# Graph gather summed in pairs of steps: two matmuls into one PSUM bank, one add per pair, the edge list padded per tile to an even number of steps

## The chip, the cores and the metric

The kernel runs on one core of a Trainium2 chip. The metric is the device time of one execution in microseconds (us); a lower time is better.

## The reference, cut to what matters

One block of a graph transformer on 12500 nodes of 256 features, fp32. The part that the change touches is the sum of messages over the 200000 edges of the first graph:

```python
xn = _layernorm(x, axis=-1)
# GCN: h = relu(batchnorm(xn @ w1.T + b1)); xw = (h @ w2.T + b2) @ w_gcn.T
msgs = xw[src] * norm[:, None]
out = jax.ops.segment_sum(msgs, dst, num_segments=n) + b_gcn
# x = x + GCN(xn) + linear attention(xn), then a GAT-gated mixture of 4 experts is added
```

`dst` is sorted. The linear attention beside the GCN (projections of `xn`, a small state per head, a second projection) and the preparation of the second graph's edge list are computed in the same stage of the kernel as this sum.

## The kernel before, in words

The program is a row of blocks, with a barrier between them: edges and first half (`load_edges`, `first_half`), rows of the table (`table_rows`), the gather with the attention (`gather_mix`), `second_norm`, the experts with the second graph (`gat_experts`, `gat_finish`), `finale`. Only `gather_mix` does other work after the change.

Nodes lie in NT = 100 tiles of TN = 125. `table_rows` writes the scaled rows `xw` to `table` in DRAM, and makes the list of **steps**. A step is 128 edges of one tile. A tile has as many steps as its edges need (`nch`, L750 and L751), and the steps of all tiles stand behind each other; `S_GCN` (L44) is the number that suffices for any edge list, rounded up. For each step there are a column of 128 source rows (`gcn_srcT`), a column of 128 destinations less the tile's first node (`gcn_dstT`) and the tile's number (`gcn_tiles`). A step of the list beyond the last edge takes its 128 pairs from a tail that `load_edges` wrote with source 0 and destination -1 (L345 and L346): it gathers row 0 of the table 128 times, and its one-hot matrix is all zeros.

`gather_mix` takes the steps in groups of 4, and two of them make a slot (`SLOTS = S_GCN // 2`, 832). The order on each engine is written out slot by slot:

- POOL (L919 to L926) issues one indirect DMA per step, 128 rows of 1 KB from `table` into `g_rows`, a ring of 4 groups. Before a group it waits until PE has done the group 4 back (`mm_s`).
- DVE `build(g)` (L1259) makes the four one-hot matrices `g_hot` of a group by comparing `gcn_dstT` with a ramp, one group ahead.
- PE `gathered(p)` (L984 to L995) waits for the one-hots and the rows of a group, and for `add_s` of the slot 4 back, and multiplies one-hot by rows for the two steps of the slot, each into its own half of one of four banks of `g_ps`. One increment of `mm_s` follows.
- DVE `add(p)` (L1263 to L1271) reads the two tile numbers into registers, waits for `mm_s`, and adds the two halves one after the other to the accumulator row `acc` of their tiles. The second add waits for the first, since both may go to the same tile.

The attention is woven in by slot number: the first half (queries, keys and values, state) takes 13 slots for each of 25 blocks (slots 0 to 336), the second half 8 slots per block from slot 337 (to 546), and the counts of the second graph's nodes (`degrees`, L1339 and L1083) 4 slots per round, to about slot 806. A sorting network of the second graph's edges runs on DVE (L1367 and L1368) beside these. In a slot DVE does `build` (every second slot), `add`, and then its piece of the other work, strictly in this order. In the first half PE's product for keys and values (L1013) waits for DVE's `k_sum` (L1281) of the block before; in the second half PE's products L1053 and L1070 wait for DVE's L1330 and L1323.

The few lines of the slot loop on DVE:

```python
for p in range(SLOTS):
    if p % 2 == 0 and p // 2 + 1 < S_GCN // 4:
        build(p // 2 + 1)
    add(p)
    ...
```

Of the kernel before, what the change touches and what calls it, by code (L numbers as in the profile page):

```python
# [10 lines left out]
ALU = mybir.AluOpType  # L11
# [4 lines left out]
D = 256  # L16
P = 128
TN = 125
NT = N // TN
# [11 lines left out]


ROUND = BATCH * HALVES


def steps_for(edges, unit):


    most = (edges + NT * P * unit) // P
    return -(-most // ROUND) * ROUND  # L40


UNIT_GCN = 1
S_GCN = steps_for(E_GCN, UNIT_GCN)  # L44
G_GCN = -(-S_GCN // P)
NE, FF = 4, 512
# [106 lines left out]
def where(eng, flag):  # L153

    return nullcontext() if flag is None else eng.If(eng.value_load(flag[:], min_val=0, max_val=1))
# [139 lines left out]
def scatter_unsorted(nc, K):  # L295

    with ExitStack() as ctx:
        scatter = Scatter(Mem(nc, ctx), "gc", K.gcn_pairs, GCN_P, K.gcn_place, K.gcn_pay)
        with nc.Block() as block:
            @block.gpsimd  # L300
            def _(pool):
                with where(pool, K.unsorted):
                    scatter.run(pool, 0, GCN_C // ROUND)

# [300 lines left out]
def table_rows(nc, K, A):  # L605
# [3 lines left out]
    with ExitStack() as ctx:  # L609
# [12 lines left out]
        G = G_GCN  # L622
        wide = P * UNIT_GCN
        ch_start, ch_end, base = (m.sb("t_" + s, [P, NT]) for s in ("start", "end", "base"))
# [24 lines left out]
        with nc.Block() as block:  # L649
# [79 lines left out]
            def _(dve):  # L729
# [13 lines left out]
                def done(ins):  # L743
                    n[0] += 1
                    ins.then_inc(t_s, 1)
                    dve.wait_ge(t_s, n[0])
# [3 lines left out]
                done(dve.tensor_scalar(nch_i[:], K.cnt[:], 1.0 / wide, (wide - 1) / (2.0 * wide), ALU.mult, ALU.add))  # L750
                done(dve.tensor_scalar(nch[:], nch_i[:], 1.0, float(UNIT_GCN), ALU.max, ALU.mult))  # L751
                done(dve.tensor_tensor_scan(ch_end[:], nch[:], nch[:], 0.0, ALU.add, ALU.bypass))
# [58 lines left out]
def gather_mix(nc, K, A):  # L811
# [9 lines left out]
    RING, HB = 4, 16  # L821
    with ExitStack() as ctx:
        m = Mem(nc, ctx)
        rows = m.sb("g_rows", [P, RING, 4, D])
        hot = m.sb("g_hot", [P, 3, 4, TN])
        ps = m.ps("g_ps", [P, 4, 2, D])
        hot_s, mm_s, add_s = (m.sem("g_" + s) for s in ("hot", "mm", "add"))
        got = [m.gather_sem(f"g_got{h}") for h in range(RING)]

# [65 lines left out]
        q = slice(0, TN)  # L895
# [18 lines left out]
        with nc.Block() as block:  # L914
# [69 lines left out]
            def _(pe):  # L984
                def gathered(p):
                    g, j = divmod(p, 2)
                    if j == 0:
                        pe.wait_ge(hot_s, g + 1)
                        pe.wait_ge(got[g % RING], 64 * (g // RING + 1))
                    if p >= 4:  # L990
                        pe.wait_ge(add_s, 2 * p - 6)
                    for b in range(2):
                        mm = pe.matmul(ps[q, p % 4, b], hot[:, g % 3, 2 * j + b], rows[:, g % RING, 2 * j + b],  # L993
                                       start=True, stop=True, skip_group_check=True)
                    mm.then_inc(mm_s, 1)  # L995

                def project_q(k, o):
# [135 lines left out]
                for p in range(SLOTS):  # L1133
                    gathered(p)
                    k, r = divmod(p - MIX1, W1)
                    if 0 <= k < NB:
                        if r in (0, 2):
                            project_q(k, r // 2)
                        elif r in (3, 5, 7, 9):
                            project_kv(k, (r - 3) // 2)  # L1140
                        elif r in (6, 8, 10, 12):
                            accumulate(k, (r - 6) // 2)
                    middle(p - MIX1 - NB * W1)
                    k, r = divmod(p - MIX2, W2)
                    if 0 <= k < NB:
                        second(k, r)
                    if 0 <= p - HIST - W3 < half * W3:
                        degrees(p - HIST - W3)
                    if p % 2 == 0:
                        next(order, None)  # L1150
# [103 lines left out]
            def _(dve):  # L1254
# [6 lines left out]
                                      ).then_inc(hot_s, 1)  # L1261

                def add(p):  # L1263
                    tiles = [dve.value_load(K.gcn_tiles[0:1, 2 * p + b:2 * p + b + 1], min_val=0, max_val=NT - 1)
                             for b in range(2)]
                    dve.wait_ge(mm_s, p + 1)
                    for b in range(2):
                        a = K.acc[q, bass.ds(tiles[b], 1), :].rearrange("p a f -> p (a f)")
                        if p or b:
                            dve.wait_ge(add_s, 2 * p + b)  # L1270
                        dve.tensor_tensor(a, a, ps[q, p % 4, b], ALU.add).then_inc(add_s, 1)  # L1271

                def q_sum(k, o):
                    n = k * KC + o
# [214 lines left out]
# [4 lines that stand above are left out]
                    k, r = divmod(p - MIX1, W1)  # L1493
                    if 0 <= k < NB:
                        if r in (1, 3):
                            q_sum(k, r // 2)
                        elif r in (4, 6, 8, 10):
                            k_sum(k, (r - 4) // 2)
                    middle(p - MIX1 - NB * W1)
                    k, r = divmod(p - MIX2, W2)  # L1500
                    if 0 <= k < NB:
                        second(k, r)
                    numbers(p - HIST + 3)
                    if 0 <= p - HIST < half * W3:
                        degrees(p - HIST)
                    if p % 2 == 0:
                        next(order, None)
                    if p >= HIST - 40 and p % 2 == 1:
                        next(after, None)
# [778 lines left out]
def program(nc, A):  # L2288
    with ExitStack() as ctx:
# [23 lines left out]
        with ExitStack() as c1:  # L2313
            m1 = Mem(nc, c1)
            K.gcn_srcT = m1.sb("gcn_srcT", [P, G_GCN * P], U32)
            K.gcn_dstT = m1.sb("gcn_dstT", [P, G_GCN * P])
            K.gcn_tiles = m1.sb("gcn_tiles", [1, G_GCN * P], I32)
            K.acc = m1.sb("acc", [P, NT, D])
            with ExitStack() as c2:
                m2 = Mem(nc, c2)  # L2320
                K.both = m2.sb("w_both", [P, KC, D])
                K.b_both = m2.sb("b_both", [P, D])
                K.hmv = m2.sb("hmv", [P, KC, 2])
                K.cnt = m2.sb("cnt", [P, NT])
                with ExitStack() as c6:
                    m6 = Mem(nc, c6)
                    K.degree = m6.sb("degree", [P, NT])
                    K.base = m6.sb("base", [P, NT])
                    load_edges(nc, m6, K, A)
                    with ExitStack() as c7:  # L2330
                        K.gcn_place = Mem(nc, c7).sb("gcn_place", [P, GCN_C], U32)
                        places(nc, K, "gc", GCN_P, GCN_C, K.gcn_tile, K.cnt, K.base, K.gcn_place, K.unsorted)
                        scatter_unsorted(nc, K)
                    first_half(nc, K, A)
                table_rows(nc, K, A)
            gather_mix(nc, K, A)
            second_norm(nc, K, A)
# [43 lines left out]
```

## Time and profile before

| What | Value |
|---|---|
| median of 3 runs | 6648.84 us (6631.96 to 6654.02) |
| the profiled execution | 6612.06 us, span 6610.4 us |
| stage of the gather, from DVE's first add to its last | 734 to 3368 us |
| PE, DVE, POOL busy over the span | 67%, 39%, 44% |
| mean granted TensorE clock | 0.737 |

The profiled execution is 37 us under the median and 20 us under the lowest of the three runs. Times are us from the span's start. Shares over the whole span say little here, since each stage has its own bound; the stage is read by itself, and inside it by the work that is woven in. PE rows carry the start of a matmul, their ends are modelled. A wait for several semaphores stands under the one that came last by the trace; "issue" is time in which the engine waited for nothing that the profile shows, "remote" a release that the profile could not place.

### The profile page before, as it was taken

Reading aid. Unit: us, or ns where it says so; the run is one execution under the profiler, and the core shown is the slowest. Engines: PE = TensorE matmul, PEld = TensorE weight load, DVE = VectorE, ACT = ScalarE, POOL = GpSimd, SP = SyncE. Lnnn points to the kernel's source line nnn. Section 1 sums busy time; section 2 is a strip of 40 time slices with the busy share of each in tenths; the row PEclk is TensorE's granted clock in tenths of the full one; section 3 lists DMA queues with packets and bytes.
Section 4 is the critical chain, followed back from the end, with each engine's and each line's share of the span. In section 5 each row is a group of like instructions: output and inputs, shape, how many; then the busy total and the mean of one; then the engine's idle time right before and its main releaser. Section 6 shows DMA issues by size and latency. Waiting matters only on the chain. (4 is left out here: it accounts for less than half of the span.)

```text
span 6610.4 us, 50389 instructions
## 1 busy us (share of the span) xinstructions
PE 4430.7 (67%) x14755; PEld 3046.5 (46%) x14755; DVE 2593.8 (39%) x5223; ACT 758.7 (11%) x1439; POOL 2901.8 (44%) x2919
## 2 busy tenths in 40 slices
PE   6998777888788887777754325764775485451264
PEld 6887544444455555666644113442443253230143
DVE  5555565565554445555554000220221121113244
ACT  1112311212000000000011001110111011010111
POOL 0000466666655556777710772334434523552300
PEclk8667989888776777777755557876876697675687
DMA  2112433333444443333465211221221121211265
GB/s 68 50 50 51 138 114 113 109 116 112 114 129 124 128 116 93 92 90 91 88 132 148 37 9 41 50 50 25 50 50 26 35 64 27 45 31 39 54 174 140
DMA packets 241863, 531.52 MB, mean 80 GB/s; under 512 B 73332, under 2 KB 147415, under 8 KB 234822
## 3 DMA queue, kind: packets, MB, share of 16 engines
q1 hardware_dynamic: 121909, 293.42, 16.4%
q0 software_dynamic: 119696, 235.05, 15.1%
q8 instruction: 115, 1.88, 0.1%
q14 instruction: 143, 1.17, 0.1%
HBM read 377.97 MB, written 150.28 MB: 80 GB/s over the span
## 5 line engine op out<-in xcount | busy, mean ns | idle before, releaser
L923 POOL DMA_INDIRECT g_rows<-table,gcn_srcT x1664 | 1707.0, 1026 | 915.9 <-issue 460.9
L1768 POOL DMA_INDIRECT n_rows<-gtab,so_own x1122 | 1081.7, 964 | 1246.6 <-DVEq L1885 905.5
L993 PE MATMUL g_ps<-g_rows,g_hot 128*125 128x256 f32 x3328 | 1082.3, 463 | 262.8 <-DVE g_hot L1259 172.0
L1716 PE MATMUL p_py<-f_w,f_hh 128*125 128x256 f32 x2688 | 723.0, 407 | 791.8 <-issue 791.6
L1271 DVE TENSOR_TENSOR acc<-acc,g_ps 125x256 f32 x1664 | 700.6, 421 | 1004.1 <-PE g_ps L993 339.1
L1716 PEld LDWEIGHTS p_py<-f_w,f_hh 128*125 128x125 f32 x2688 | 539.2, 201 | 994.9 <-issue 932.3
L993 PEld LDWEIGHTS g_ps<-g_rows,g_hot 128*125 128x125 f32 x3328 | 702.8, 229 | 514.2 <-issue 210.4
L1909 DVE TENSOR_TENSOR p_ob<-p_py,p_xb 125x512 f32<-125x512 f32 x168 | 114.6, 691 | 1971.0 <-remote 1031.1
L1710 PE MATMUL p_ph<-f_xfT,f_w 128*128 128x500 f32 x1344 | 652.9, 628 | 258.6 <-issue 190.3
L1710 PEld LDWEIGHTS p_ph<-f_xfT,f_w 128*128 128x128 f32 x1344 | 270.2, 201 | 604.6 <-issue 601.3
L1938 ACT ACTIVATE f_hh<-p_ph,f_b 128x500 f32<-128x500 f32 x336 | 224.3, 677 | 1955.7 <-remote 1143.1
L462 PE MATMUL a_pdeg<-so_x 125*125 125x100 bf16 x1600 | 378.9, 412 | 23.8 <-DVE so_x L537 23.8
L462 PEld LDWEIGHTS a_pdeg<-so_x 125*125 125x125 bf16 x1600 | 379.3, 330 | 32.7 <-issue 30.0
L1013 PE MATMUL m_pb<-m_area 128*125 128x512 f32 x400 | 239.5, 729 | 170.7 <-DVE m_area L1281 160.6
L1710 PE MATMUL z_ph<-f_xfT,f_w 128*128 128x500 f32 x256 | 121.9, 633 | 262.6 <-DMA f_xfT<-xfT_d 148.0
L1083 PEld LDWEIGHTS m_pa<-m_area 128*125 128x125 bf16 x1024 | 268.7, 326 | 52.7 <-issue 31.5
L1083 PE MATMUL m_pa<-m_area 128*125 128x100 bf16 x1024 | 266.9, 396 | 28.0 <-DVE m_area L1339 24.4
L673 POOL DMA_INDIRECT t_pair<-gcn_pairs,t_first_i x13 | 12.5, 958 | 618.3 <-DVE t_node L774 614.7
L1259 DVE TENSOR_TENSOR g_hot<-iota,gcn_dstT 128x500 f32<-128x500 f32 x416 | 280.3, 674 | 6.6 <-PEq L82 6.4
L1013 PEld LDWEIGHTS m_pb<-m_area 128*125 128x125 f32 x400 | 82.3, 221 | 261.4 <-DVE m_area L1281 183.6
L537 DVE TENSOR_TENSOR so_x<-so_own,gcn_node 125x2000 bf16<-125x2000 bf16 x100 | 120.0, 1200 | 210.0 <-PE a_pdeg L462 207.1
L1710 PEld LDWEIGHTS z_ph<-f_xfT,f_w 128*128 128x128 f32 x256 | 52.6, 208 | 325.0 <-DMA f_xfT<-xfT_d 148.1
(322 smaller groups left out, 4183.4 us busy)
## 6 DMA issues: line engine op xcount, KB each, us to landing
o_d<-p_ob SPq DMA_DIRECT2D x21, 1920.0 KB
z_ob<-o_d SPq DMA_DIRECT2D x21, 1920.0 KB
g_rows<-table,gcn_srcT POOLq DMA_INDIRECT x1664
n_rows<-gtab,so_own POOLq DMA_INDIRECT x1122
gout<-n_o SPq DMA_DIRECT2D x11, 1224.0 KB
xnT_d<-a_xnT SPq DMA_DIRECT2D x25, 500.0 KB, 3.0
m_area<-xnT_d SPq DMA_DIRECT2D x25, 500.0 KB
qT_d<-m_area SPq DMA_DIRECT2D x25, 500.0 KB
```

Source lines behind the costliest of these rows:

```text
L462: mm = pe.matmul(pdeg[q], on[0:c, r % 2, :, b], ot[0:c, r % 2, :, b], start=r == 0 and b == 0, stop=r == rounds - 1 and b == HB - 1)
L537: dve.tensor_tensor(out[0:c, r % 2], number[0:c, 0:width], ids[0:c, r * HB:(r + 1) * HB].unsqueeze(1).to_broadcast([c, width, HB]), ALU.is ...
L923: pool.indirect_dma_start(out=rows[:, g % RING, j], out_offset=None, in_=K.table, in_offset=bass.IndirectOffsetOnAxis(ap=K.gcn_srcT[:, 4 * ...
L993: mm = pe.matmul(ps[q, p % 4, b], hot[:, g % 3, 2 * j + b], rows[:, g % RING, 2 * j + b], start=True, stop=True, skip_group_check=True)
L1013: pe.matmul(pb[q], xnT[:, k % 2, c, j * TN:(j + 1) * TN], wkv[:, c].rearrange("p a o -> p (a o)"), start=c == 0, stop=False, skip_group_ch ...
L1083: mm = pe.matmul(pa[q, 0:NT], on[:, r % 2, :, b], ot[:, r % 2, :, b], start=r == 0 and b == 0, stop=r == half - 1 and b == HB - 1)
L1259: dve.tensor_tensor(hot[:, g % 3], K.iota[:, q].unsqueeze(1).to_broadcast(shape), K.gcn_dstT[:, 4 * g:4 * g + 4].unsqueeze(2).to_broadcast ...
L1271: dve.tensor_tensor(a, a, ps[q, p % 4, b], ALU.add).then_inc(add_s, 1)
L1710: mm = pe.matmul(ph[:, o, 0:BN], self.w1[:, e, c, o * P:(o + 1) * P], self.xfT[:, s, c], start=c == 0, stop=c == KC - 1)
L1716: mm = pe.matmul(py[0:TN, e % 2, j // 2, (j % 2) * D:(j % 2 + 1) * D], self.hh[:, e % 2, c, j * TN:(j + 1) * TN], self.w2[:, e, c], start= ...
L1768: pool.indirect_dma_start(out=rows[:, c % 3, j], out_offset=None, in_=K.gtab, in_offset=bass.IndirectOffsetOnAxis(ap=K.gat_src[:, c * W + ...
L1938: act.activation(X.hh[:, e % 2, o], ph[:, o, 0:BN], ACT.Gelu, bias=X.b1[:, e, o:o + 1]).then_inc(hh_s, 1)
```

## The change

A tile's steps are padded to an even number (`UNIT_GCN = 2`), so that the two steps of a slot always belong to one tile. PE accumulates both in one bank of `g_ps` (`start` on the first matmul, `stop` on the second), and DVE reads one tile number and makes one add per slot. The bound on the number of steps grows by the padding, and its rounding goes from 16 to 4: 1764 steps and 882 slots in place of 1664 and 832. The numbers of the woven-in work are unchanged, so it ends at the same slot as before.

```diff
 def steps_for(edges, unit):
     most = (edges + NT * P * unit) // P
-    return -(-most // ROUND) * ROUND
-UNIT_GCN = 1
+    return -(-most // GROUP) * GROUP
+UNIT_GCN = 2
...
-        ps = m.ps("g_ps", [P, 4, 2, D])
+        ps = m.ps("g_ps", [P, 4, 512])
...
                     if p >= 4:
-                        pe.wait_ge(add_s, 2 * p - 6)
+                        pe.wait_ge(add_s, p - 3)
                     for b in range(2):
-                        mm = pe.matmul(ps[q, p % 4, b], hot[:, g % 3, 2 * j + b], rows[:, g % RING, 2 * j + b],
-                                       start=True, stop=True, skip_group_check=True)
+                        mm = pe.matmul(ps[q, p % 4, 0:D], hot[:, g % 3, 2 * j + b], rows[:, g % RING, 2 * j + b],
+                                       start=b == 0, stop=b == 1, skip_group_check=True)
                     mm.then_inc(mm_s, 1)
...
                 def add(p):
-                    tiles = [dve.value_load(K.gcn_tiles[0:1, 2 * p + b:2 * p + b + 1], min_val=0, max_val=NT - 1)
-                             for b in range(2)]
+                    tile = dve.value_load(K.gcn_tiles[0:1, 2 * p:2 * p + 1], min_val=0, max_val=NT - 1)
                     dve.wait_ge(mm_s, p + 1)
-                    for b in range(2):
-                        a = K.acc[q, bass.ds(tiles[b], 1), :].rearrange("p a f -> p (a f)")
-                        if p or b:
-                            dve.wait_ge(add_s, 2 * p + b)
-                        dve.tensor_tensor(a, a, ps[q, p % 4, b], ALU.add).then_inc(add_s, 1)
+                    a = K.acc[q, bass.ds(tile, 1), :].rearrange("p a f -> p (a f)")
+                    if p:
+                        dve.wait_ge(add_s, p)
+                    dve.tensor_tensor(a, a, ps[q, p % 4, 0:D], ALU.add).then_inc(add_s, 1)
```

How many of the steps hold edges follows from the reference's `dst`: the hundred tiles have 1859 to 2121 edges each, which makes 1612 steps of 128 before and 817 pairs, 1634 steps, after. The other steps, 52 before and 130 after, are padding at the end of the list.

The order of DVE's instructions in the first half, around `k_sum` (`SCALAR_TENSOR_TENSOR m_area<-m_pb,m_area`), before:

```order
L1264 TENSOR_LOAD gcn_tiles
L1264 ISA x2
L1264 TENSOR_LOAD gcn_tiles
L1264 ISA x2
L1271 ISA [waits g_add,g_mm]
L1271 TENSOR_TENSOR acc<-acc,g_ps 125x256
L1271 ISA [waits g_add]
L1271 TENSOR_TENSOR acc<-acc,g_ps 125x256
L1281 SCALAR_TENSOR_TENSOR m_area<-m_pb,m_area 125x256 [waits m_ke]
```

and of the change:

```order
L1265 TENSOR_LOAD gcn_tiles
L1265 ISA x2
L1270 ISA [waits g_add,g_mm]
L1270 TENSOR_TENSOR acc<-acc,g_ps 125x256
L1280 SCALAR_TENSOR_TENSOR m_area<-m_pb,m_area 125x256 [waits m_ke]
```

One load, two register instructions, one wait and one add have gone from in front of `k_sum`: 10 instructions of an add have become 5.

The same engine in the second half, where it has PE's output of a block to add (L1330, of the change L1329), before:

```order
L1330 TENSOR_TENSOR m_area<-m_area,m_pb 125x512 [waits m_o,m_in_x1]
L1259 TENSOR_TENSOR g_hot<-iota,gcn_dstT 128x500 [waits g_mm]
L1264 TENSOR_LOAD gcn_tiles
L1264 ISA x2
L1264 TENSOR_LOAD gcn_tiles
L1264 ISA x2
L1271 ISA [waits g_add,g_mm]
L1271 TENSOR_TENSOR acc<-acc,g_ps 125x256
L1271 ISA [waits g_add]
L1271 TENSOR_TENSOR acc<-acc,g_ps 125x256
L1330 TENSOR_TENSOR m_area<-m_area,m_pc 125x512 [waits m_o]
```

and of the change:

```order
L1329 TENSOR_TENSOR m_area<-m_area,m_pb 125x512 [waits m_o,m_in_x1]
L1260 TENSOR_TENSOR g_hot<-iota,gcn_dstT 128x500 [waits g_mm]
L1265 TENSOR_LOAD gcn_tiles
L1265 ISA x2
L1270 ISA [waits g_add,g_mm]
L1270 TENSOR_TENSOR acc<-acc,g_ps 125x256
L1329 TENSOR_TENSOR m_area<-m_area,m_pc 125x512 [waits m_o]
```

Nothing has changed places; between the two halves of the output there is one add in place of two.

## Rows read from the trace of the kernel before

**Rows 1.** Costliest groups of the page: busy, mean ns; idle before, releaser.
```profile
L923 POOL DMA_INDIRECT g_rows<-table,gcn_srcT x1664 | 1707.0, 1026 | 915.9 <-issue 460.9
L993 PE MATMUL g_ps<-g_rows,g_hot 128*125 128x256 f32 x3328 | 1082.3, 463 | 262.8 <-DVE g_hot L1259 172.0
L1271 DVE TENSOR_TENSOR acc<-acc,g_ps 125x256 f32 x1664 | 700.6, 421 | 1004.1 <-PE g_ps L993 339.1
```

**Rows 2.** Stretches of the stage: busy time by engine, granted clock, DMA share, GB/s.
```profile
core 0: us, PE busy (x) PEld busy (x) DVE busy (x) ACT busy (x) POOL busy (x), PEclk, DMA share, GB/s
734.00:1762.00 1028.00, 808.18 (x2686) 479.81 (x2684) 622.30 (x1307) 199.97 (x491) 689.17 (x677) 0.87 0.38 113
1762.00:2546.00 784.00, 655.85 (x2064) 416.60 (x2064) 380.58 (x753) 19.96 (x35) 428.33 (x428) 0.74 0.44 121
2546.00:3295.00 749.00, 561.42 (x2061) 487.80 (x2062) 419.95 (x778) 0.00 (x0) 545.15 (x516) 0.76 0.34 90
```

**Rows 3.** Waits of POOL, 734 to 1762: total us, times, longest.
```profile
POOL g_rows L923 <- issue: 187.3, 606, 0.9
POOL g_rows L923 <- PE g_ps L993: 104.6, 48, 8.5
POOL g_rows L923 <- remote: 46.9, 23, 2.9
```

**Rows 4.** Waits of POOL, 1762 to 2546.
```profile
POOL g_rows L923 <- PE g_ps L993: 236.7, 49, 13.9
...
POOL g_rows L923 <- remote: 4.3, 3, 2.0
```

**Rows 5.** Waits of POOL, 2546 to 3295.
```profile
POOL g_rows L923 <- remote: 40.6, 15, 3.6
POOL g_rows L923 <- PE g_ps L993: 17.4, 22, 3.9
```

**Rows 6.** Stretches at the end, edges up to about 3271, then padding (columns as in rows 2).
```profile
3200.00:3260.00 60.00, 48.32 (x188) 43.08 (x189) 39.70 (x75) 0.00 (x0) 45.74 (x42) 0.81 0.32 91
3276.00:3336.00 60.00, 27.52 (x75) 19.30 (x74) 21.63 (x48) 0.00 (x0) 40.41 (x42) 0.64 0.97 77
```

**Rows 7.** The gather's line: duration ns min/median/max, first and last start us.
```profile
L923 POOL DMA_INDIRECT g_rows<-table,gcn_srcT x1664: 940/946/2827, 721.5 to 3343.3; - x185
```

**Rows 8.** The line of the register loads of tile numbers, columns as in rows 7.
```profile
L1264 DVEq TENSOR_LOAD <-gcn_tiles x1664: 1/302/1381, 728.3 to 3365.8; - x185
L1264 DVEq FUSED_REGOPS  x1664: 1/190/1399, 728.7 to 3366.1; - x185
```

**Rows 9.** Timeline of DVE in the padding: start, us, line; idle before.
```profile
3320.09 0.99 DVE L1271 TENSOR_TENSOR acc<-acc,g_ps 125x256 f32 x2 [0.49 <-issue]
...
3322.12 0.99 DVE L1271 TENSOR_TENSOR acc<-acc,g_ps 125x256 f32 x2 [1.03 <-issue]
```

**Rows 10.** Waits of PE, 734 to 1762.
```profile
PE m_pb L1013 <- DVE m_area L1281: 160.6, 56, 10.4
```

**Rows 11.** Waits of PE, 1762 to 2546.
```profile
PE m_pb L1070 <- DVE m_area L1323: 43.7, 13, 5.7
PE m_pb L1053 <- DVE m_area L1330: 21.6, 9, 2.9
```

**Rows 12.** Timeline of DVE, the node counts: two of its long gaps.
```profile
2637.93 0.99 DVE L1271 TENSOR_TENSOR acc<-acc,g_ps 125x256 f32 x2 [8.60 <-remote]
...
2732.36 0.99 DVE L1271 TENSOR_TENSOR acc<-acc,g_ps 125x256 f32 x2 [7.16 <-remote]
```

**Rows 13.** Line 1271 between such gaps: adds in two overlapping stretches (DVE busy, x).
```profile
2638.00:2732.20 94.20, 26.87 (x64) 0.75 0.32 91
2669.00:2761.60 92.60, 27.67 (x66) 0.79 0.32 91
```

**Rows 14.** Timeline of PE, first half: one round of keys and values.
```profile
1234.20 1.98 PE L1013 MATMUL m_pb<-m_area 128*125 128x512 f32 x4 [0.22 <-issue]
...
1239.40 1.98 PE L1013 MATMUL m_pb<-m_area 128*125 128x512 f32 x4 [0.22 <-DVE m_area L1281]
```

More of the change, by code:

```diff
@@ L33 @@
 ROUND = BATCH * HALVES
+GROUP = 4
 def steps_for(edges, unit):
     most = (edges + NT * P * unit) // P
-    return -(-most // ROUND) * ROUND
-UNIT_GCN = 1
+    return -(-most // GROUP) * GROUP
+UNIT_GCN = 2
 S_GCN = steps_for(E_GCN, UNIT_GCN)
```

## The prediction

> **What bounds the kernel now.** First the page's costliest groups [rows 1]: the gather is POOL's 1664 indirect DMAs, PE's product and DVE's 1664 adds. None of the three engines fills the stage from 734 to 3368 us, so I read the stage by stretches [rows 2]: the attention's first half (A, 1028 us, slots 0 to 336), its second half (B, 784 us, to slot 546), the node counts (C, 749 us, to slot 806), and the rest. All other stages stay as they are.
>
> POOL has a floor that no other engine can lower. In A its 677 DMAs took 689.2 us [rows 2], and between them lie 187.3 us of "issue" [rows 3]: 876.5 us, 1.29 us a step or 2.59 us a slot of two. What is left of A, 104.6 + 46.9 = 151.5 us [rows 3], is POOL waiting until PE frees a group of rows. The same rest is 236.7 + 4.3 = 241.0 us in B [rows 4] and 40.6 + 17.4 = 58.0 us in C [rows 5]. These waits are all that a faster DVE can win.
>
> Who makes them? In A, a round of keys and values that runs well takes 1239.40 - 1234.20 = 5.20 us for two slots, with PE idle for 0.22 us [rows 14]. That is 2.60 us a slot, POOL's floor, and it is PE's own work; there a cheaper add wins nearly nothing. The average slot of A takes 1028 / 337 = 3.05 us. The difference comes from times in which PE waits for DVE [rows 10], from a TensorE clock that is not always 2.4 GHz (mean 0.87 in A, 0.74 and 0.76 in B and C, the rest at 1.2 GHz [rows 2]), and from the way in which the loop catches up: DVE then passes slots at 3322.12 - 3320.09 = 2.03 us [rows 9], and behind each add stands the piece of attention that PE wants next. In B this order is a chain: PE waits for L1323 and L1330 of DVE [rows 11], and both stand behind adds.
>
> At the end of the list the bound is another one. The steps of padding gather one row 128 times. Before them the DMA engines are busy 0.32 of the time at 91 GB/s, in them 0.97 at 77 GB/s, while POOL issues 42 DMAs in 60 us either way [rows 6]. A step is 131 KB, so padding costs 131 / 77 = 1.70 us a step, and it is bound by the DMA engines. Neither POOL's nor DVE's speed counts there.
>
> **The change part by part.**
>
> *More steps.* There are 100 more: 22 with edges and 78 of padding. The 22 with edges come after slot 806, where nothing is woven in, at POOL's price with no wait: 0.946 us [rows 7] and about 0.30 us of issue (187.3 / 606 [rows 3]), 1.25 us each, 27 us. The 78 of padding cost 1.70 us each, 133 us. Together **+160 us**. The bounds: 100 x 1.25 = 125 us if padding cost no more than any gather, 100 x 1.70 = 170 us if all were as slow as padding. The slower value is the one measured at that place.
>
> *Half the adds.* Of 421 ns each [rows 1], 1664 become 882: 329 us less of busy DVE. Beside each add that goes, so does a register load, 302 + 190 ns [rows 8], about 0.6 us with what lies between. DVE's catching-up slot of 2.03 us should become about 1.1 us (an estimate: one load and one add of two). This is the whole gain, and it counts only as far as it removes POOL's waits:
>
> - A: of 151.5 us I take 0.55, **-83 us**. PE waits 160.6 us for `k_sum` in 56 pieces [rows 10]. Each piece loses the 0.42 us of an add and its wait of some 0.15 us, which is 32 us; the rest should come from catching up faster.
> - B: the waits of 241.0 us cannot all go, as PE is busy 655.9 of 784 us [rows 2]; its 128 us idle are the cap. I take half, **-64 us**. The waits of rows 11 (43.7 + 21.6 = 65 us) say the same.
> - C: of 58.0 us I take 0.6, **-35 us**. DVE has long gaps here, 8.60 and 7.16 us [rows 12], and they return after 64 and 66 adds [rows 13], that is every 32 or 33 slots, some 350 DVE instructions. If they belong to DVE's instruction stream, half the instructions make half the gaps.
>
> Each of these may be nothing at all, or the whole of it: 0 to 151.5 + 128 + 58 = 337 us. I sit a little over the middle, because DVE's share falls in every slot, yet PE and POOL stand right behind it (2.4 us of PE a slot in A, 808 / 337, against the floor of 2.59).
>
> *One PSUM bank, two matmuls accumulated.* The products have the same shape and number per step. I cost this at nothing; it is covered in A and B only while PE has idle time (220 and 128 us [rows 2]). If accumulating cost PE more, B would show it first. PE's wait for `add_s` keeps its distance of four slots.
>
> *The list.* `table_rows` turns 14 blocks of indices in place of 13, under its other work: nothing. Gathers do not get shorter with fewer adds, I assume; at most they fall from a mean of 1.026 [rows 1] to 0.946 us [rows 7], which belongs to the upper bound of the gain.
>
> The sum: 160 - 83 - 64 - 35 = -22 us. On the profiled execution's 6612 us that is 6590. This execution lies 37 us under the median of 6649; against the median the forecast is 6649 - 22 = **6627 us**.
>
> **The rivals.**
>
> *The long gaps stay (slower).* At a long gap the profile names no release that fits, and several engines stand still together. If PE or the memory makes the gaps, not DVE's instructions, they come as often as before, and the clock falls after them as before. Then C wins nothing, A wins the 32 us of the cheaper way to `k_sum`, and B the 65 us of rows 11: 97 us against 160, **+63 us, 6712 us**. The side is decided by whether fewer than 160 us of POOL's 450 us of waits go. For it: PE's clock and its own work stay as they are, and in rows 14 PE alone keeps the pace. Against it: the even spacing of the gaps in DVE's stream [rows 13].
>
> The Trainium skill, "Runtime: NRT & Kernel Launch", section "Instruction fetch mechanics", says that an engine fetches its next block of instructions while it executes the current one, so that the cost of crossing a block is mostly hidden. By that rule fewer DVE instructions would not thin the gaps out, and the time would be that of this rival. The 8.60 us of rows 12 are not hidden, but they do not say what they are.
>
> *Nearly all waits go (faster).* DVE at 1.1 us a slot lets the loop run on POOL's floor: A -120, B -100, C -50, against +160: **-110 us, 6539 us**. For it: the floor is reached in a good round [rows 14]. Against it: PE in B, busy for 84%.
>
> *Padding costs what a gather costs.* +125 in place of +160 gives **-57 us, 6592 us**. Rows 6 speak against it.
>
> That the change does not halve the adds can be left out: the order of the instructions shows it.
>
> **How the numbers follow.** A difference of 0.3%, 20 us, is about what a measurement of this kernel can tell from none. The forecast has a chance of 0.47 (from -90 to +40 us around it; of this 0.24 is faster by over 20 us, 0.16 within 20 us, 0.07 slower), the long gaps that stay 0.38 (0.30 slower, 0.07 within, 0.01 faster), the two faster rivals 0.10 and 0.05. That makes 0.40 faster, 0.23 the same, 0.37 slower. The predicted time is that of the forecast. The range goes from the fast rival, 6540, to a little beyond the slow one, 6730; its own range alone would be 6560 to 6690.
>
> **What would show it.** Right: adds x882; the gathers of the last 220 us at 77 GB/s and a DMA share near 0.97; A near 945 us, B near 720, C near 715 to slot 806; POOL's waits for PE in these at some 270 us; the stage ending about 22 us earlier. DVE's gaps in C of over 5 us at double distance would prove the step on C, gaps at every 32 slots would refute it. Wrong: A and B that do not get shorter while DVE's busy share falls (then PE or its clock is the bound), a PE row of L993 with a longer mean than its 463 ns, or padding at another rate.

## The result and the profile after

The change makes the kernel **slower by 0.8%**: 6690.28 us median (6 runs, 6683.3 to 6704.16) against 6641.02 (6 runs, 6625.95 to 6654.02), ratio 1.0077 with a 95% interval of 1.0057 to 1.0098. A second comparison, in a later session, gave 1.0089 [1.0073, 1.0106]. The forecast was 6627 us, a little faster: the time is inside its range and on the wrong side of no change. The nearest case was the rival in which the long gaps stay, 6712 us.

The costliest groups of the page after, which answer to [rows 1] (busy, mean ns; idle before):

```profile
L924 POOL DMA_INDIRECT g_rows<-table,gcn_srcT x1764 | 1787.2, 1013 | 907.9 <-issue 488.5
L994 PE MATMUL g_ps<-g_rows,g_hot 128*125 128x256 f32 x3528 | 1140.6, 463 | 324.3 <-issue 155.5
L1270 DVE TENSOR_TENSOR acc<-acc,g_ps 125x256 f32 x882 | 370.0, 419 | 1412.5 <-PE g_ps L994 843.9
```

DVE's adds fell from 700.6 to 370.0 us, its idle time before them rose from 1004.1 to 1412.5. POOL's idle time, which is what counts, is 907.9 us in place of 915.9. The change took 331 us of work from an engine, and the same engine now waits 408 us longer.

The stretches A, B, C of [rows 2], cut at the same slots (337 and 547) of the program after, and the padding (busy us of PE, PE's weight loads, DVE, ACT, POOL; granted clock, DMA share, GB/s):

```profile
737.00:1754.00 1017.00, 796.80 (x2663) 480.04 (x2661) 478.12 (x969) 199.82 (x491) 675.18 (x670) 0.87 0.38 113
1754.00:2438.00 684.00, 589.72 (x2079) 388.21 (x2079) 288.64 (x543) 19.96 (x35) 422.20 (x422) 0.81 0.49 138
2438.00:3197.00 759.00, 558.13 (x2060) 488.08 (x2061) 310.51 (x517) 0.00 (x0) 546.30 (x524) 0.75 0.32 91
3222.00:3441.00 219.00, 112.86 (x256) 74.12 (x256) 45.24 (x96) 0.00 (x0) 116.64 (x123) 0.66 0.96 75
```

| | before | after | forecast |
|---|---|---|---|
| A, slots 0 to 336 | 1028 | 1017 | 945 |
| B, to 546 | 784 | 684 | 720 |
| C, to 806 | 749 | 759 | 715 |
| edges after slot 806 | 0 | 25 | 27 |
| padding | 74 | 219 | 74 + 133 |

B alone won much, and more than I gave it. A won 11 us and C nothing, though DVE's busy time fell by 144 and 109 us in them.

POOL's waits after, for A, B and C in turn, beside [rows 3 to 5] (us, times, longest):

```profile
POOL g_rows L924 <- issue: 184.4, 595, 0.8
POOL g_rows L924 <- PE g_ps L994: 79.2, 42, 6.7
POOL g_rows L924 <- remote: 78.5, 33, 3.2
...
POOL g_rows L924 <- PE g_ps L994: 115.6, 36, 12.8
...
POOL g_rows L924 <- remote: 32.4, 13, 2.8
...
POOL g_rows L924 <- remote: 54.5, 19, 3.9
POOL g_rows L924 <- PE g_ps L994: 7.7, 11, 3.2
```

In A 151.5 us of waiting became 157.7, and only the name of the releaser moved, from "PE" to "remote". In B 241.0 became 148.0, in C 58.0 became 62.2. That is the result in short: POOL waits 93 us less in B and no less elsewhere, and 170 us of steps are added. The stage is 70 us longer (2634 us before, 2704 after). The two profiled executions are 90 us apart and the medians 49, because the profiled execution of before was faster than all its other runs; 17 of the 90 us lie behind the stage.

### The profile page after: what moved, and what is told of

The parts are those of the page before. It is cut to its first block and busy times, and to the rows that moved or that the text cites. A ratio compares the mean times of both kernels' runs of the same rounds, so it can differ in the third digit from the quotient of the medians.

```text
span 6700.2 us, 47091 instructions
## 1 busy us (share of the span) xinstructions
PE 4450.2 (66%) x14957; PEld 3082.6 (46%) x14957; DVE 2275.1 (34%) x4471; ACT 759.0 (11%) x1439; POOL 2984.3 (45%) x3020
## 5 line engine op out<-in xcount | busy, mean ns | idle before, releaser
L924 POOL DMA_INDIRECT g_rows<-table,gcn_srcT x1764 | 1787.2, 1013 | 907.9 <-issue 488.5
L994 PE MATMUL g_ps<-g_rows,g_hot 128*125 128x256 f32 x3528 | 1140.6, 463 | 324.3 <-issue 155.5
L994 PEld LDWEIGHTS g_ps<-g_rows,g_hot 128*125 128x125 f32 x3528 | 754.1, 230 | 586.5 <-issue 306.0
L1270 DVE TENSOR_TENSOR acc<-acc,g_ps 125x256 f32 x882 | 370.0, 419 | 1412.5 <-PE g_ps L994 843.9
L1014 PE MATMUL m_pb<-m_area 128*125 128x512 f32 x400 | 236.8, 722 | 178.8 <-DVE m_area L1280 149.6
L1260 DVE TENSOR_TENSOR g_hot<-iota,gcn_dstT 128x500 f32<-128x500 f32 x441 | 297.1, 674 | 6.6 <-PEq L83 6.4
L1709 PEld LDWEIGHTS z_ph<-f_xfT,f_w 128*128 128x128 f32 x256 | 52.3, 206 | 323.2 <-DMA f_xfT<-xfT_d 148.0
```

Of the source, the lines that this page charges most:

```text
L924: pool.indirect_dma_start(out=rows[:, g % RING, j], out_offset=None, in_=K.table, in_offset=bass.IndirectOffsetOnAxis(ap=K.gcn_srcT[:, 4 * ...
L994: mm = pe.matmul(ps[q, p % 4, 0:D], hot[:, g % 3, 2 * j + b], rows[:, g % RING, 2 * j + b], start=b == 0, stop=b == 1, skip_group_check=True)
L1014: pe.matmul(pb[q], xnT[:, k % 2, c, j * TN:(j + 1) * TN], wkv[:, c].rearrange("p a o -> p (a o)"), start=c == 0, stop=False, skip_group_ch ...
L1260: dve.tensor_tensor(hot[:, g % 3], K.iota[:, q].unsqueeze(1).to_broadcast(shape), K.gcn_dstT[:, 4 * g:4 * g + 4].unsqueeze(2).to_broadcast ...
L1270: dve.tensor_tensor(a, a, ps[q, p % 4, 0:D], ALU.add).then_inc(add_s, 1)
L1709: mm = pe.matmul(ph[:, o, 0:BN], self.w1[:, e, c, o * P:(o + 1) * P], self.xfT[:, s, c], start=c == 0, stop=c == KC - 1)
```

## The experiments

They ran in four sessions on four chips, so each is given as a ratio to the kernel before in the same session. On three chips that kernel takes 6595 to 6630 us, on the second session's chip 5471. Stage times come from windows cut at the same slots.

**The list alone** (before_list), without the gain: the kernel before, with

```diff
-UNIT_GCN = 1
-S_GCN = steps_for(E_GCN, UNIT_GCN)
+UNIT_GCN = 2
+S_GCN = 1764
```

> The kernel before with the change's longer list alone (tiles padded to pairs, 1764 steps), each step added by itself as before. This is the price of the list without its gain. Theory (the terms add up): 160 to 200 us over the kernel before, the padding at 3.4 us a slot, the edges at 25 to 30 us, A, B and C as before. Rival (the price of the list and the gain of fewer adds hang together): less than 130 us, or A, B or C move by over 30 us.

Measured: 6794.05 us, ratio 1.0256 [1.0239, 1.0273], which is +166 us. A, B, C: 1016, 781, 754 (before in that session, in the one profile of it: 1040, 777, 752). The terms add up: the list costs 166 us, and the changed kernel (6684.0 in that session) wins 110 of it back with fewer adds.

**The gain alone**, without most of the list: the changed kernel with 1664 steps (1634 with edges and 30 of padding, all edges there).

```diff
-S_GCN = steps_for(E_GCN, UNIT_GCN)
+S_GCN = 1664
```

> The pairing alone, with the number of steps of the kernel before: 1664 steps, of which 1634 hold edges and 30 are padding. Against the change, 100 steps of padding are gone. If padding is bound by the DMA engines at 1.70 us a step, 6690 - 170 = 6520 us. If padding costs what the traces show for a plain issue on POOL, 1.25 us, 6690 - 125 = 6565 us. Against the kernel before (6641) the first theory makes the pairing alone worth 121 us.

Measured: 6505.57 us, ratio 0.9804 [0.9764, 0.9844], 124 us faster. A 1003, B 687, C 768. Expected were 121 us if padding is bound by the DMA engines. So the idea pays; what spoils it is 100 steps of padding. The capacity of the list is set for the worst case, and with these edges 1634 steps are filled; a list this short isn't safe for other edges.

**Padding that reads different rows.** The tail's source column gets the numbers 0, 97, 194, ... by partition in place of one row's number (the weight matrix of padding stays zero).

```diff
-pool.memset(tail[:, 0:1], 0).then_inc(chain, 1)
+pool.iota(tail[:, 0:1], [[1, 1]], base=0, channel_multiplier=97).then_inc(chain, 1)
```

> The change, with the same spread padding. If the repeated row makes the gather slow, 130 x 0.45 = 58 us go: 6632 us, level with the kernel before. If not, 6690 us.

> The kernel before, with padding that gathers 128 different rows in place of row 0 128 times. If the repeated row makes the gather slow, the DMA share in the padding falls from 0.97 to about 0.32, a step there costs 1.25 to 1.3 us in place of 1.70, and 52 x 0.45 = 23 us go: 6618 us. If something else at the end of the list is slow, no change: 6641 us.

Measured: on the changed kernel 6640.61 us, ratio 1.002 [1.0001, 1.0039] in place of 1.0077; on the kernel before 6623.68, ratio 0.9997 [0.9974, 1.002]. The padding of the changed kernel with one row, and then with spread rows, is here:

```profile
3260.00:3320.00 60.00, 31.10 (x72) 20.30 (x70) 12.89 (x27) 0.00 (x0) 36.25 (x38) 0.56 0.98 77
```

```profile
3240.00:3400.00 160.00, 71.88 (x204) 51.39 (x203) 37.91 (x86) 1.28 (x1) 91.22 (x95) 0.70 0.30 85
```

With one row the DMA engines are busy 0.98 of the time at 77 GB/s, with spread rows 0.30 at 85 GB/s. The whole padding falls from 219 us to 176 us for 130 steps, 1.68 to 1.35 us a step, the second being near POOL's own price of 1.29. That is 43 us for the 58 expected. For the kernel before the expectation failed: the share fell as foreseen, to 0.25 in 60 us of its padding, but its 52 steps took as long as before (74 and 76 us), where 23 us should have gone. In the profile of before DVE and PE were still catching up with POOL while the padding was gathered, which may be why; no run shows it.

**Half of PE's product left out.** The changed kernel with the first of the two matmuls alone; the second step's rows are missing from the sum.

```diff
-                    for b in range(2):
+                    for b in range(1):
...
-                                       start=b == 0, stop=b == 1, skip_group_check=True)
+                                       start=True, stop=True, skip_group_check=True)
```

> The change with only the first of the two products of a slot: the second step of each pair is left out of the sum, its gather and its one-hot stay. It asks what bounds the first half and the node counts now that DVE is lighter. If PE and its clock are the bound, slots fall to POOL's floor of 2.6 us: the first half (1017 us) by 100 us or more, the node counts (759 us) by 50 us. If POOL waits for something else (a long gap that comes with DVE's instruction stream), both stay within 30 us.

Measured: 6677.95 us in one run. Its A, B, C:

```profile
737.00:1726.00 989.00, 695.96 (x1994) 362.92 (x1994) 476.21 (x970) 199.68 (x491) 681.59 (x671) 0.80 0.39 117
1726.00:2430.00 704.00, 634.39 (x1654) 359.91 (x1654) 287.84 (x544) 19.96 (x35) 420.22 (x422) 0.60 0.48 134
2430.00:3181.00 751.00, 479.23 (x1540) 404.86 (x1541) 309.72 (x517) 0.00 (x0) 548.17 (x517) 0.50 0.32 91
```

A quarter of PE's instructions gone, and C stands at 751 us with a granted clock of 0.50, all of it at the lower level of 1.2 GHz. In C neither PE's work nor its clock is the bound. A loses 28 us. With half the adds and half of this product gone A still takes 989 us, 120 us over what POOL's DMAs and their issue take, so the amount of that work is not what holds it. B became 20 us longer, although a fifth of PE's instructions had gone: its granted clock stood at 0.60 in place of 0.81. So less work for PE does not make B shorter either.

**More instructions.** Do the long gaps come with an engine's instruction stream? The changed kernel with 16 waits more per slot (they are met at once; two make one instruction, so 8 instructions), on PE (pe_more) and then on DVE (dve_more):

```diff
                     mm.then_inc(mm_s, 1)
+                    for _ in range(16):
+                        pe.wait_ge(hot_s, 1)
```

> The change with 8 more instructions per slot on PE's sequencer (waits that have long been met, 51 ns each in the traces, 0.4 us a slot together). In the node counts (759 us) PE's long gaps came every 18 slots in the change and every 22 in the run with half the products, about as often as PE was sent a new block of instructions. If the gaps come with PE's instruction stream, they come every 12 or 13 slots, and the node counts grow by 40% of the gaps' 218 us, by 60 to 90 us, the first half likewise by 30 us or more. If they come with DVE's stream or with time, spacing and stage stay: within 20 us of 759, and the whole within 20 us of 6690.

> The change with 8 more instructions per slot on DVE's sequencer instead, of the same kind. If the long gaps come with DVE's instruction stream (the prediction's step on the node counts), they come every 8 or 9 slots in place of 18, and the node counts grow by 80 us or more. If they come with PE's stream, the spacing stays at 18 slots and the whole within 20 us of 6690.

Measured, on the chip on which the kernel before takes 5471 us: ratios 1.0013 [1.0, 1.0027] and 1.0043 [1.0026, 1.006]. As a test of the streams it is **inconclusive**: on this chip the long gaps, DVE's waits for no release that fits, are missing in C, with 8 instructions more on either engine. What it shows is worth more, A, B, C of the kernel with PE's waits added:

```profile
736.00:1628.00 892.00, 761.43 (x2667) 453.89 (x2667) 482.10 (x971) 199.93 (x491) 687.91 (x671) 0.95 0.43 129
1628.00:2191.00 563.00, 522.25 (x2076) 336.89 (x2075) 288.02 (x543) 19.96 (x35) 427.37 (x422) 0.91 0.60 167
2191.00:2898.00 707.00, 594.09 (x2059) 504.49 (x2060) 314.40 (x518) 0.00 (x0) 549.33 (x518) 0.74 0.33 97
```

and its waits in A, of POOL and of PE for `k_sum`:

```profile
POOL g_rows L924 <- issue: 200.4, 658, 0.3
POOL g_rows L924 <- PE g_ps L994: 4.0, 13, 0.3
...
PE m_pb L1016 <- DVE m_area L1282: 3.9, 12, 0.5
```

A is 892 us, POOL's floor of 671 DMAs and their issue and next to nothing more, with the instructions that took 1017 us elsewhere and eight more a slot. POOL waits 4.0 us in place of 157.7. PE waits 3.9 us for `k_sum` in place of 149.6. In dve_more, with eight more instructions a slot on DVE, A is 899 us and POOL waits 4.6. So nearly all of A's waits that I priced as DVE's came with the chip, and not with the number of DVE's instructions. This is shown for kernels with half the adds; the kernel before was timed on this chip (5471 us) but not profiled, and whether its A is as short is not shown.

**A second load of a tile's number**, which nothing uses, and the two edits together (1664 steps, spread padding) ran beside them:

> The change with the second register load back in front of the add (its value isn't used): 0.6 us more of DVE's sequencer per slot, one add as in the change. If the attention's second half (784 us before, 684 us after) was won because DVE's slots are on its chain, about half of it comes back: 720 to 735 us. First half and node counts, where DVE was not the bound, stay within 15 us of 1017 and 759.

> Pairs with 1664 steps, and the 30 steps of padding on 128 different rows. 30 x (1.70 - 1.25) = 14 us less than 6506 us, 6492 us. It is the candidate for the fastest kernel.

Measured: 1.0022 [1.0009, 1.0036] with the load, B 576 us against the 563 above and 562 with the two edits together. So 13 us came back where 36 to 51 were expected, on a chip where all of B is shorter. And 5286.02 us, ratio **0.9667** [0.9643, 0.9691], for the two edits together, the fastest kernel of this study. The 14 us expected of the spread rows can't be read from it, as the 0.9804 with one row is from another chip.

**The controls.** Neither kernel had a profile from the fast chip, so both ran again unedited:

> The changed kernel, nothing edited. An earlier set of runs came from a chip on which the kernel before takes 5471 us in place of 6641, and there the changed kernel was run only with things added. Theory (the waits of A and C that the change did not win are long stalls of the chip on which it was timed first, no work of DVE): where the stalls are rare, A is near POOL's floor with the change and without, B still wins, C wins little, and the longer list costs its 160 to 180 us all the same, so the ratio to the kernel before is again 1.000 to 1.008. Rival (the change did win in A and C, and the stalls ate it): on the chip with few stalls the ratio is well under 1, below 0.99.

> The kernel before, nothing edited, for its stages. Theory (long stalls, not DVE, make POOL's waits in A): on a chip with few stalls A is 880 to 910 us, the 873 us of POOL's floor and a little, though all 1664 adds are there. Rival (DVE's adds make them): A is 950 us or more, against 892 of the kernels with half the adds on the same chip. B in either: 640 to 680 us against 563 to 584.

They ran on a chip of the slower kind, so neither theory is tested: how the change stands on the fast chip is known only through kernels with something added. As controls they serve: ratio 1.0089; A 1020, B 664, C 758 after; A 1040, B 777, C 752 before.

**What B won: add, load or PSUM?** First (two_adds) the second DVE operation put back, of the same shape (the maximum of the accumulator with itself), with PE's wait for `add_s` counted accordingly:

```diff
+                    dve.tensor_tensor(a, a, a, ALU.max).then_inc(add_s, 1)
+                    dve.wait_ge(add_s, 2 * p + 1)
                     dve.tensor_tensor(a, a, ps[q, p % 4, 0:D], ALU.add).then_inc(add_s, 1)
```

> The changed kernel with one more DVE operation of the same shape per slot: it takes the maximum of the accumulator with itself, which leaves the values as they are. So two operations and two waits of DVE per slot, but one load of a tile's number and one PSUM bank. If what the change won in B is the add itself, half or more of the difference between one and two adds comes back: 50 to 90 us more than the changed kernel, nearly all in B. If it was the register load and its queue, this one costs under 30 us. A and C: no change by over 20 us in the theory that DVE bounds neither.

Measured: ratio 1.0105 [1.0089, 1.0122], 9 us over the changed kernel, B 677 us. So the second add by itself, beside one load, is not what B won. Then three kernels that cut it finer: the long list with two products and two adds but one load, whose edit is shown; the changed kernel with a second load, as above; and the changed kernel with load and operation both put back.

```diff
-                    tiles = [dve.value_load(K.gcn_tiles[0:1, 2 * p + b:2 * p + b + 1], min_val=0, max_val=NT - 1)
-                             for b in range(2)]
+                    tile = dve.value_load(K.gcn_tiles[0:1, 2 * p:2 * p + 1], min_val=0, max_val=NT - 1)
```

> The kernel before with the longer list (as in before_list) and one load of the tile's number per slot in place of two; still two products in two halves of a bank and two adds, each with its wait. before_list took B 781 us and 166 us over the kernel before. If the load that goes is what B won, this one has B near the 677 us of two_adds and stands 60 to 80 us over the kernel before. If it is the accumulation of two products in PSUM (one result for DVE to read in place of two), B stays near 780 us and the whole at +150 or more. If it is the add after all, both this and two_adds would have to win, each in part: B 700 to 750.

> The changed kernel with a second load of a tile's number per slot, which nothing uses. If the load is what B won: B 740 to 780 us, the whole 60 us or more over the changed kernel (ratio 1.018 to 1.026 to the kernel before). If not: B 665 to 700, ratio 1.009 to 1.012. If only load and add together fill the room that DVE has in B, also under 1.012.

> The changed kernel with both put back, a second DVE operation per slot and a second load, so DVE has per slot all it had before; only the accumulation in PSUM remains of the change. If DVE's work of whatever kind is what B won, this gives all of it back: B 760 to 785, 100 us or more over the changed kernel, ratio 1.024 to 1.027, as before_list. If the accumulation in PSUM is the gain, B stays under 700 and the ratio under 1.014.

| per slot on DVE | B, us | clock | ratio of the kernel |
|---|---|---|---|
| 2 loads, 2 adds, two products apart (before_list) | 781 | 0.75 | 1.0256 |
| 2 loads, 2 operations, accumulated in PSUM (two_adds_load2) | 774 | 0.73 | 1.0213 [1.0167, 1.0258] |
| 1 load, 2 adds, two products apart (list_one_load) | 718 | 0.79 | 1.0134 [1.0096, 1.0172] |
| 2 loads, 1 add (load2_again) | 711 | 0.79 | 1.0103 [1.0071, 1.0135] |
| 1 load, 2 operations, accumulated in PSUM (two_adds) | 677 | 0.83 | 1.0105 |
| 1 load, 1 add (the changed kernel) | 664, 684 | 0.83, 0.81 | 1.0089, 1.0077 |

Most of it is DVE's work: with the accumulation kept, load and operation put back give back nearly all of B (774 us). It doesn't add up by length. From that 774, taking away the operation wins 63 us, taking away the load 97, and taking away both 90 to 110. Accumulating in PSUM is worth 7 us by the first two rows and 41 by the third and fifth (718 and 677), which also differ in it alone, but for what the second operation reads. These are single profiles from two chips, and four profiles of kernels with the change's slots have B from 664 to 687 us. So a share of PSUM in the gain isn't excluded, where DVE has one load. With both put back B is where DVE's work alone would have it (774 in 760 to 785), at a ratio a little under the expected 1.024 to 1.027; the other two fall between the theories, 718 where each piece wins in part (700 to 750), and 711 between the 665 to 700 and the 740 to 780 of the load. Product and clock in B, before, with both put back, and after:

```profile
L993 PE MATMUL g_ps<-g_rows,g_hot 128*125 128x256 f32 x840 | 295.8, 499 | 21.8 <-DVE g_hot L1259 21.2 <-issue 0.6
```

```profile
L994 PE MATMUL g_ps<-g_rows,g_hot 128*125 128x256 f32 x840 | 292.1, 494 | 11.9 <-issue 11.9
```

```profile
L994 PE MATMUL g_ps<-g_rows,g_hot 128*125 128x256 f32 x840 | 273.2, 468 | 5.7 <-issue 4.8 <-DVE g_hot L1260 0.9
```

The same product takes 499 ns a matmul before and 468 after, and the granted clock of the stretch rose with it from 0.74 to 0.81. Of the 100 us of B, PE's busy time gave 655.9 - 589.7 = 66 and its idle time 34.

## Why the prediction was wrong, step by step

- **More steps, +160: right.** Measured alone, 166 us. The edges took 25 us for 27, the padding 219 for 74 + 133 = 207, at 75 GB/s and a share of 0.96. The trace of before held it, in a stretch of 60 us.
- **A, -83: the step that failed first.** I took 0.55 of POOL's 151.5 us of waits as DVE's, since PE "waits 160.6 us for `k_sum`". After the change PE waits 149.6 us at the same place, in 29 pieces for 56:

```profile
PE m_pb L1014 <- DVE m_area L1280: 149.6, 29, 12.8
```

  The small pieces went, as worked out, and the time stayed in fewer, longer ones. The row told who was late, and nothing of whether that engine was working or stood still. DVE stood still: in A it waits at its adds for no release that fits, 105.9 us before and 189.3 after, and one such wait of 9.05 us nearly fills one of PE's long waits for `k_sum`:

```profile
DVE acc L1271 <- remote: 105.9, 30, 7.9
```

```profile
DVE acc L1270 <- remote: 189.3, 50, 9.1
```

```profile
1704.34 0.42 DVE L1270 TENSOR_TENSOR acc<-acc,g_ps 125x256 f32 x1 [9.05 <-remote]
...
1705.15 2.07 PE L1014 MATMUL m_pb<-m_area 128*125 128x512 f32 x2 [9.04 <-DVE m_area L1280]
```

  On the slower chips A took 1016 to 1040 us (1027 in the mean) in five profiles with DVE's work whole, 1003 to 1020 (1012) in four with the change's slots, so the change is worth some 15 us there in place of 83; on the chip without these gaps A took 892. A good round of 5.20 us [rows 14] and POOL's floor said that DVE was no bound; I set the difference down to DVE's way of catching up.
- **B, -64: right in kind, too small.** Measured -100 and -113 in two sessions. The cap that I set, PE's 128 us of idle time, was wrong, since PE's busy time is no constant: 66 us came from it, at a higher granted clock. That DVE's load and add are to be priced by their length was wrong as well, as the table shows.
- **C, -35: failed.** The step was that the long gaps go with DVE's instructions, so that half of them would make half the gaps. DVE's waits for no release that fits, in C before and then after:

```profile
DVE acc L1271 <- remote: 125.0, 25, 9.6
```

```profile
DVE acc L1270 <- remote: 161.6, 28, 11.5
```

  and two of the gaps after, with the adds in the stretch from one to the next (of the views: timeline, then windows with DVE's line 1270 alone):

```profile
2732.56 0.42 DVE L1270 TENSOR_TENSOR acc<-acc,g_ps 125x256 f32 x1 [9.27 <-remote]
...
2843.86 0.42 DVE L1270 TENSOR_TENSOR acc<-acc,g_ps 125x256 f32 x1 [8.04 <-remote]
```

```profile
2733.00:2843.80 110.80, 15.54 (x37) 0.78 0.32 91
```

  Thirty-seven slots lie between these two, with one of 7.09 us (at 2786.59) half way: a gap every 18 or 19 slots. Nor were they 32 slots apart before. I had taken one series of gaps at a time, and the two stretches of [rows 13] overlap: between the two gaps of [rows 12] lies a third,

```profile
2668.90 0.99 DVE L1271 TENSOR_TENSOR acc<-acc,g_ps 125x256 f32 x2 [8.29 <-remote]
```

  10 slots after the first and 22 before the second, so before they came every 16 slots in the mean. Half as many would be one in 32; they stayed about as frequent. What the gaps are stays open. They are there on the chips on which the kernel before takes some 6600 us, and in C of the kernels that ran on the faster chip this wait of DVE's has no row at all. The queue that brings DVE its instructions (the one that grew when dve_more gave DVE more of them) moved a fifth fewer blocks after the change, in the whole program, before and then after:

```profile
q14 instruction: 143, 1.17, 0.1%
```

```profile
q14 instruction: 115, 0.94, 0.0%
```

  The gaps did not become fewer with them, nor with PE's instructions cut by a quarter (175.7 us in 29 pieces), and on the faster chip dve_more had 170 such blocks and none of these gaps in C. So a block of instructions to be fetched doesn't make a gap by itself. Whether fetching is what is slow on the slower chips, no run shows.
- **The sum.** Forecast 160 - 182 = -22. Measured, on one chip, 166 - 110 = +56: the cost right to 4%, the gain three fifths of what I took. In the two profiles of the result B gave 36 us more than forecast, which by luck hid a third of what A and C fell short (72 and 45 us). The error is one habit, to take a middling share of each wait: three guesses near one half hide that two of them were next to no gain at all.
- **The rival that stays slower** put A at -32, B at -65, C at 0, and +63 in all; A gave -11 and B -100. Its word for A, the small pieces alone, was near; for B it was too low. The section "Instruction fetch mechanics" of the Trainium skill ("Runtime: NRT & Kernel Launch"), by which fewer DVE instructions would not thin the gaps out, pointed to the right side; the runs agree with that consequence, and do not show that its reason is the one.
- **The rival on padding** (what a gather costs, 125 us for the list) is false for one row gathered 128 times and near for spread rows: 1.35 us a step, 43 us less than with one row, which would make the list's 166 us some 123 (an estimate).

## What to carry to other kernels

An engine's wait row says who was late, not that the late one was busy: before pricing a wait as work, look at a good round of the same stretch; if that runs on the floor, as here, see in the late engine's own rows whether it stood still; where it did, making it faster won 15 us of 83. Padding that points at one address isn't free: give the dummy entries different rows, and size the list by what it must hold, since here the added padding cost some 140 us and the merged adds won 110. And where an engine's busy time changes with its granted clock, that busy time is no cap on the gain.

## What was not expected of the hardware

- **One row read 128 times by an indirect gather** kept the DMA engines busy 0.96 of the time at 75 GB/s; other rows in the same steps 0.30 at 85 GB/s. 1.68 us a step against 1.35. The bytes are the same, so they don't tell it: the share of the DMA engines beside GB/s does.
- **The same kernel on another chip takes 5471 us in place of some 6630**, with the same instructions. In the changed kernel with PE's waits added, against the changed kernel on the slower chip, what follows the stage is shorter too (2330 us in place of some 3250), what comes before it is not (736 us in place of 737), and the padding hardly (213 us in place of 219). A tuned kernel's waits can be the machine's. In which way the chips differ isn't known here.
- **The granted clock moved with the work.** B stood at 0.73 to 0.75 with DVE full, at 0.79 to 0.83 with a piece of its work gone, at 0.60 with half the products left out as well, and at 0.90 to 0.93 on the faster chip; C at 0.50 with half the products and yet as long as at 0.75. Which of the two, clock or pace, led the other isn't shown.
- **Open**: whether the change would be a gain or a loss on the fast chip. With a little added it stood at 1.0013 to 1.0043 there, so the unedited one should be at or below that, near no change.
